# The first eight expert blocks planned and loaded one batch earlier, and the weight splits and the bias fold moved into the last loop body

## The reference, cut to what matters

```
x = x + linear_attention(layernorm(x))            # 16 heads of width 8, prefix sums of Chebyshev polynomials
f = layernorm(x)
f = f + causal_attention(layernorm(f, g1, b1))    # 16 heads, softmax
h = layernorm(f, g2, b2)                          # 8192 tokens x 128
logits = h @ gate_W + gate_b                      # 8 experts
top_v, top_i = top_k(logits, 2);  w = softmax(top_v)
for e in range(8):
    y_e = gelu(h @ exp_W1[e] + exp_b1[e]) @ exp_W2[e] + exp_b2[e]     # 128 -> 512 -> 128
    out += w_full[:, e] * y_e                     # w_full is zero except at the two chosen experts
x = x + f + out
```

## Time and profile before

| | us |
|---|---|
| median of three runs | 1423.27 |
| the three runs | 1413.66, 1423.27, 1428.15 |
| profiled execution, first to last instruction (span) | 1342.0 |
| of it the pipeline over batches, to PE's last product of it | 0 to 1022 |
| PE without work between the pipeline and the first block | 1022 to 1040.5 |
| expert blocks, first hidden product to the second layer's last product | 1043 to 1293.5 |
| last scatters, pairs, sum and store | 1293.5 to 1342 |

### The profile page before, as it was taken

One profiled execution on the slowest core, in us unless ns is written; L12 is line 12 of the kernel. 1 busy time (PEld: TensorE's weight loads), 2 busy tenths in 40 slices (PEclk: granted clock), 3 DMA queues, 4 the chain that ended last, 5 costly groups with the idle time before them and its releaser, 6 DMA issues.

```text
span 1342.0 us, 27933 instructions
## 1 busy us (share of the span) xinstructions
PE 1131.7 (84%) x8883; PEld 706.3 (53%) x8883; DVE 1101.1 (82%) x2555; ACT 938.9 (70%) x1859; POOL 845.8 (63%) x1105
## 2 busy tenths in 40 slices
PE   4576799899999999899998999998891999999950
PEld 1233355554655545555555555554460788888840
DVE  4648889899999999999999999877615788888845
ACT  3243387687877978878777687686664799999940
POOL 3776656778778787777877777532323266666660
PEclk8657799999999999999999999899995899999985
DMA  9131221414325133242341322413431222222239
GB/s 223 40 90 49 53 73 34 122 54 85 90 42 122 66 73 94 58 101 79 61 110 44 83 78 54 109 57 80 152 127 58 79 82 76 93 79 82 67 142 375
DMA packets 84436, 121.91 MB, mean 91 GB/s; under 512 B 15270, under 2 KB 66522, under 8 KB 80002
## 3 DMA queue, kind: packets, MB, share of 16 engines
q1 hardware_dynamic: 70978, 98.07, 27.5%
q0 software_dynamic: 9088, 17.33, 3.9%
q10 hardware_dynamic: 4224, 4.72, 1.0%
HBM read 63.96 MB, written 57.46 MB: 90 GB/s over the span
## 4 chain that ended last, share of the span: by engine, by line
PE 49%; DVE 17%; POOL 12%; issue 9%; ACT 8%; DMA 4%; POOLq 1%; ACTq 0%; SPq 0%; DVEq 0%
PE front L1621 8%; PE back L1633 8%; DVE nm L619 7%; PE back L1487 5%; POOL xg L1217 4%; PE scores L1468 4%; PE front L1353 4%; ACT pr L1006 3%; PE maxima L1428 3%; POOL F L1173 2%; PE scores L1470 2%; DMA stack<-pairs 2%; DVE front L570 2%; POOL F L1174 2%; PE maxima L1430 2%
## 5 line engine op out<-in xcount | busy, mean ns | idle before, releaser
L619 DVE TENSOR_REDUCE nm<-maxima 128x1 f32<-128x384 f32 (+3 forms) x704 | 419.4, 632 | 48.1 <-PE maxima L1430 44.2
L1006 ACT ACTIVATE pr<-scores 128x384 f32<-128x384 f32 (+1 forms) x768 | 373.5, 524 | 105.6 <-PE scores L1470 88.3
L1428 PE MATMUL maxima<-stack 65*128 65x128 bf16 (+2 forms) x768 | 199.5, 283 | 38.0 <-DVE nm L619 34.9
L1468 PE MATMUL scores<-stack 65*128 65x384 bf16 (+2 forms) x768 | 205.9, 280 | 21.7 <-ACT pr L1006 18.1
L1217 POOL DMA_INDIRECT xg<-rows,sloti x128 | 133.0, 1039 | 130.0 <-ACT rows L1027 43.4
L1430 PE MATMUL maxima<-stack 128*128 128x128 bf16 x1024 | 181.4, 225 | 1.5 <-DVE nm L619 1.0
L1470 PE MATMUL scores<-stack 128*128 128x128 bf16 x1024 | 181.1, 223 | 0.0
L1487 PE MATMUL back<-pr,vaug 128*9 128x512 f32 (+3 forms) x2048 | 179.9, 452 | 0.0
L1292 POOL DMA_INDIRECT pairs<-xs x104 | 111.1, 1069 | 78.8 <-DVE xs L852 52.1
L1468 PEld LDWEIGHTS scores<-stack 65*128 65x128 bf16 x768 | 75.6, 98 | 135.6 <-ACT pr L1006 93.7
L1428 PEld LDWEIGHTS maxima<-stack 65*128 65x128 bf16 x768 | 75.2, 99 | 129.2 <-DVE nm L619 85.1
(11 more groups left out here) (219 smaller groups left out, 2466.9 us busy)
## 6 DMA issues: line engine op xcount, KB each, us to landing
stack<-spread SPq DMA_DIRECT2D x32, 400.0 KB
spread<-qs SPq DMA_DIRECT2D x96, 128.0 KB
spread<-ks SPq DMA_DIRECT2D x96, 128.0 KB
stack<-spread SPq DMA_DIRECT2D x32, 384.0 KB
xs<-xg SPq DMA_DIRECT2D x39, 272.0 KB, 2.8
stack<-pairs SPq DMA_DIRECT2D x8, 1024.0 KB, 16.7
stack<-in_consts SPq DMA_DIRECT2D x4, 1280.0 KB
xg<-xs SPq DMA_DIRECT2D x17, 272.0 KB, 2.3
```

Source lines behind the costliest of these rows:

```text
L619: v.tensor_reduce(nm[:, h:h + heads, t], ring(n)[:, 0:heads * (t + 1) * P].rearrange("p (h n) -> p h n", h=heads), AX.X, ALU.max, negate=T ...
L1006: a.activation(pr[:, n % PR, 0:width], ringE[n % 2][:, 0:width], ACT.Exp).then_inc(W.exp_ready, 1)
L1428: k.matmul(ring(n)[:, at:at + t * P], qst[p][0:OPEN_ROWS, h, own], kst[p][0:OPEN_ROWS, h, 0:t * P], start=(j == 0), stop=True, skip_group_ ...
L1468: k.matmul(dst[:, at + P:at + T - t * P], kst[p][0:OPEN_ROWS, h, own], qst[p][0:OPEN_ROWS, h, (t + 1) * P:T], start=(t == tiles[0]), stop= ...
```

## The change

1. **Plan in two halves.** After batch 14's slots DVE plans eight blocks (`EARLY`) from the counts so far, rounded down, so that they are full of rows of batches 0 to 14 (`early_plan`, in the body before the last, slot 65). The other 31 are planned as before, less what is taken (`late_plan`), after the last body and behind block 0's weights and `second_x(0)`.
2. **Rows loaded early.** SP loads six blocks (`AHEAD`) at the head of the last body, behind the filler rows and ahead of batch 15's store; two more behind that store; from block 8 on it waits for the second plan and for batch 15's rows.
3. **Splits earlier.** In the last body ACT makes six experts' first parts ahead of `apply3` (before: none), DVE seven second parts ahead of `gate_top` (before: one); none is left behind the body. `w1_sb` gets its own place over `F`, so that DVE's second parts no longer overwrite it.
4. **Bias fold later.** The 32 products leave the scores of batch 15 and stand in the last body on PE: 12 behind `output2`, 6 behind the gate, 14 behind the ranks. DVE adds them up at its slot 66.
5. **Waits.** PE no longer waits for the whole plan and all 16 second parts; it waits for `b1_ready` ahead of the first hidden product.

```diff
-        w1_sb = qst[0].rearrange("p h n -> p (h n)").bitcast(F32).rearrange("p (e n) -> p e n", e=E)
+        w1_sb = nc.alloc_sbuf_tensor_at("w1_raw", [P, E, HID], F32, offset=place["F"])
...
-        SPLIT_DVE, SPLIT_ACT = (20, 36, 45, 52), (17, 24, 58, 64, 76, 80, 84, 87)
+        SPLIT_DVE, SPLIT_ACT = (6, 8, 10, 12, 14, 16, 18, 34), (2, 4, 6, 8, 10, 12, 22, 40)
+        FOLD_PE = ((10, 12), (44, 6), (60, E * HC - 18))
...
             def body(t, b, m, g, h, f, p, w):
+                if t == B - 1:
+                    sp.wait_ge(W.plan_ready, 1)
+                    sp.wait_ge(W.tail_set, 16 * (2 * E + 1))
+                    sp.wait_ge(W.rows_free, B)
+                    sp.wait_ge(W.acc_set, 16 * (B - 1))
+                    for i in range(AHEAD):
+                        load_rows(i)
...
-            sp.wait_ge(W.plan_ready, 1)
             sp.wait_ge(W.acc_set, 16 * B)
-            sp.wait_ge(W.rows_free, B + 1)
-            for i in range(BLOCKS):
-                at = sp.value_load(plani[0:1, 0, i:i + 1], min_val=0, max_val=E * REGION)
+            for i in range(AHEAD, BLOCKS):
+                if i == EARLY:
+                    sp.wait_ge(W.plan_ready, 2)
+                    sp.wait_ge(W.rows_free, B + 1)
                 if i >= XT:
                     sp.wait_ge(added[i % 2], added_by(i - XT))
-                sp.dma_start(xt[i % XT], xg[bass.ds(at, NB), :].rearrange("(p t) c -> p (t c)", t=QT)).then_inc(xt_loaded[i % XT], 16)
+                load_rows(i)
...
+            def early_plan():
+                v.memset(taken[:, 1:4, :], 0.0).then_inc(W.p_step, 1)
+                v.tensor_scalar(number, cst[:, C_BN:C_BN + BLOCKS], float(NB), None, ALU.mult).then_inc(W.p_step, 1)
+                dve.wait_ge(W.p_step, 3)
+                whole_blocks(3, -0.5 + 0.5 / NB)
+                v.tensor_scalar(upto_taken, upto, float(EARLY), None, ALU.min).then_inc(W.p_step, 1)
+                place_blocks(9, 0, EARLY)
...
+                    if t == B - 2 and n == 65:
+                        early_plan()
+                    if t == B - 1 and n == 66:
+                        first_bias()
...
+            dve.wait_ge(W.plan_ready, 1)
             now = dve.value_load(plani[0:1, 1, 0:1], min_val=0, max_val=E - 1)
             take_w1(0, now)
             second_x(0)
+            late_plan()
...
-                if b == B - 1 and n >= TILES - E * HC:
-                    fold_bias(n - (TILES - E * HC))
...
+                    if b is None and t is not None:
+                        for i, (place, many) in enumerate(FOLD_PE):
+                            if n == place:
+                                first = sum(m for _, m in FOLD_PE[:i])
+                                for j in range(first, first + many):
+                                    fold_bias(j)
...
-            pe.wait_ge(W.plan_ready, 1)
-            pe.wait_ge(W.wl_ready, 2 * E)
...
+                if n == 0:
+                    pe.wait_ge(W.b1_ready, 1)
```

More of the change, by code:

```diff
@@ L254, in block_kernel @@
         mine = lambda k: flat[:, (XT + 1) * QT * RW + k * T:(XT + 1) * QT * RW + (k + 1) * T]
-        scraps = pr[:, 0, :]
-        at_least = x2t[:, :, :].rearrange("p t d -> p (t d)")[:, 0:BLOCKS * E].rearrange("p (n e) -> p n e", e=E)
-        plan = scraps[:, 0:BLOCKS * 4].rearrange("p (k n) -> p k n", k=4)
+        planned = ha[:, :, :].rearrange("p t d -> p (t d)")
+        at_least = outT[:, 0:BLOCKS * E].rearrange("p (n e) -> p n e", e=E)
+        plan = planned[:, 120:120 + BLOCKS * 4].rearrange("p (k n) -> p k n", k=4)
+        taken = planned[:, 280:280 + 4 * E].rearrange("p (k e) -> p k e", k=4)
         gel = [mine(k) for k in range(GS)]
@@ L702, in second_weights, with first_bias @@
                                 w2p[0][:, e * HC:(e + 1) * HC, :], ALU.subtract).then_inc(W.wl_ready, 1)
+            def first_bias():
+                dve.wait_ge(W.b1_mm, 1)
+                v.tensor_tensor(b1p[:, :], X[:, 0:E * HC], col[:, V_EB:V_EB + E * HC], ALU.add).then_inc(W.b1_ready, 1)
+            count, full, upto = (nblk[:, i, :] for i in range(3))
+            upto_taken, next_taken, per_expert, at_first = (taken[:, i, :] for i in range(4))
+            expert, behind, first_row, number = (plan[:, i, :] for i in range(4))
@@ new lines, in whole_blocks @@
+            def whole_blocks(done, rounding):
+                v.tensor_tensor(count, filled_to[:, :], cst[:, C_RG:C_RG + E], ALU.subtract).then_inc(W.p_step, 1)
+                dve.wait_ge(W.p_step, done + 1)
+                v.tensor_scalar(count, count, 1.0 / NB, rounding, ALU.mult, ALU.add).then_inc(W.p_step, 1)
+                dve.wait_ge(W.p_step, done + 2)
+                v.tensor_scalar(full, count, HALF, HALF, ALU.add, ALU.subtract).then_inc(W.p_step, 1)
+                dve.wait_ge(W.p_step, done + 3)
+                v.tensor_tensor_scan(upto, one[:, 0:1].to_broadcast((P, E)), full, 0.0, ALU.mult, ALU.add).then_inc(W.p_step, 1)
+                v.tensor_scalar(per_expert, full, -float(NB), float(REGION), ALU.mult, ALU.add).then_inc(W.p_step, 1)
+                dve.wait_ge(W.p_step, done + 5)
@@ new lines, in place_blocks @@
+            def place_blocks(done, ahead, many):
+                own, cut = at_least[:, 0:many, :], slice(0, many)
+                v.tensor_tensor(own, cst[:, C_BN:C_BN + many].unsqueeze(2).to_broadcast((P, many, E)),
+                                upto.unsqueeze(1).to_broadcast((P, many, E)), ALU.is_ge).then_inc(W.p_step, 1)
+                dve.wait_ge(W.p_step, done + 1)
+                v.tensor_reduce(expert[:, cut], own, AX.X, ALU.add).then_inc(W.p_step, 1)
+                dve.wait_ge(W.p_step, done + 2)
+                v.tensor_tensor(own, own, per_expert.unsqueeze(1).to_broadcast((P, many, E)), ALU.mult).then_inc(W.p_step, 1)
+                v.tensor_scalar(plani[:, 1, ahead:ahead + many], expert[:, cut], float(E - 1), None, ALU.min).then_inc(W.p_step, 1)
+                dve.wait_ge(W.p_step, done + 4)
+                v.tensor_reduce(behind[:, cut], own, AX.X, ALU.add).then_inc(W.p_step, 1)
+                dve.wait_ge(W.p_step, done + 5)
+                v.scalar_tensor_tensor(first_row[:, cut], behind[:, cut], at_first[:, 0:1], number[:, cut], ALU.add, ALU.add).then_inc(W.p_step, 1)
+                dve.wait_ge(W.p_step, done + 6)
+                v.tensor_scalar(plani[:, 0, ahead:ahead + many], first_row[:, cut], float(E * REGION), None, ALU.min).then_inc(W.plan_ready, 1)
@@ new lines, in late_plan @@
+            def late_plan():
+                dve.wait_ge(W.p_step, 16)
+                whole_blocks(16, 0.5 - 0.5 / NB)
+                v.tensor_tensor(upto, upto, upto_taken, ALU.subtract).then_inc(W.p_step, 1)
+                v.scalar_tensor_tensor(per_expert, next_taken, float(NB), per_expert, ALU.mult, ALU.add).then_inc(W.p_step, 1)
+                v.tensor_scalar(at_first, upto_taken, float(NB), None, ALU.mult).then_inc(W.p_step, 1)
+                dve.wait_ge(W.p_step, 24)
+                place_blocks(24, EARLY, BLOCKS - EARLY)
@@ L857, in _ @@
             second_x(0)
+            late_plan()
             for i in range(BLOCKS + 2):
                 for c in range(HC):
+                    if c == 0 and i + 1 == EARLY:
+                        dve.wait_ge(W.plan_ready, 2)
                     if c == 0 and i + 1 < BLOCKS:
```

44 lines of the change are left out of this document (10 added, 34 removed).

## The result

The changed kernel ran in 1406.23 us in the median of 8 runs (1401.52 to 1412.06), the kernel before in 1421.74 (8 runs, 1413.66 to 1428.15): a ratio of 0.9897, interval 0.9866 to 0.9929. Two later comparisons gave 0.9958 (0.9931 to 0.9985) and 0.9912 (0.9879 to 0.9944); the mean of the three is 0.992, some 11 us. Forecast: 1408, 14.9 us less.

What follows compares the result with a forecast made beforehand. The expert blocks were taken as PE-bound, their start held by a chain of waits for batch 15's rows. Block 0 15.9 us earlier, less 1.0 for the late plan, gives 14.9: 1423.3 to 1408 us, range 1400 to 1418.

Steps and rivals of the forecast that it cites:

- The early rows start the blocks: Block 0: its rows are there in time; first hidden product at 1027.2 instead of 1043.08, 15.9 us earlier.
- Rival 3: SP's head waits end late, so early rows don't start the blocks; gain shrinks to 2 us, 1421; chance 0.04.
- The fold leaves the scores: Batch 15's scores: without the 32 fold products on PE, ACT's `hn` is done 3.3 us earlier, at 1001.5.
- POOL is late next: Batch 15's first POOL work stands behind batch 14's dispatches, so starts only 2.0 us earlier (bounds 0.4 and 3.3).
- The splits on this path … I take 0: Batch 15's body: six first parts on ACT hidden, seven second parts on DVE cost 0 (bounds 0 and 0.7 us).
- rival 4: Beside the blocks, DVE's copies hold up POOL's batch 15 dispatches, making block 8's rows late: slower; chance 0.04.
- The last 14 fold products 4.7 us: PE, behind the ranks and ahead of block 0: three products slow, eleven fast, 4.7 us, to 1024.8.
- The late plan 1.0 us: DVE ahead of block 1: block 1 begins 7.6 us after block 0, before 6.65; cost 1.0 us (bounds 0.4 and 2).
- Behind that, nothing: Behind block 1's start: batch 15's dispatches, the scatters, the moved store and block 8's load cost nothing more.
- the smaller gain: PE at half clock through the last 14 products, POOL free no earlier than 1006.2: 11.7 us, 1412; chance 0.16.

Runs made afterwards that it cites:

- second execution of before: The kernel before, unchanged, profiled a second time; time 1410.95 us, span 1409.1 us.
- no early rows: Changed kernel, but first blocks' rows load only when all of batch 15's rows have landed, late plan ahead of block 0; ratio to before 1.0029.
- the execution that I summed on: The kernel before, unchanged, in the profiled execution the prediction started from; span 1342.0 us.
- all moved: Changed kernel with fold in 26 and 6, splits moved off the root, late plan spread, block 0's expert read before the gate; 1400.24 us, ratio 0.9874.

## Why the prediction held, and which steps of it did not

Against the second execution of before, the three executions of the changed kernel have the first product 15.2 us earlier (mean 54.7 against 69.9), block 3 12.2 earlier, the end 11.5 earlier. The forecast had 15.9, then 14.9 and 14.9.

1. *The early rows start the blocks: right, and without them there is no gain* ("no early rows"). SP issued the six loads from 1072.45 to 1078.40, block 0's first: 14.5 us ahead of its transposes, where a load took 2.71 us from issue to landing in the earlier trace rows. Rival 3 is out.

```profile
1072.45 5.95 SPq L390 DMA_DIRECT2D xs<-xg  x6
```

2. *The fold leaves the scores, `hn` 3.3 earlier: right in kind, 2.2 in the mean.* The three executions with the fold in the scores have `hn` at 30.2 in the mean, the ten without at 28.0. The single ones overlap (28.6 to 31.3 against 26.5 to 30.3), so the runs don't tell 2.2 from the 3.3.
3. *"POOL is late next": wrong.* The residual sum waits for DVE's `x2t` (3.74 us above), as the row of before also said (4.09) and I argued away. I also counted the landing, 2.3 to 3.7 us, from the end of the last dispatch's row (1003.70) where it counts from the start (1002.74), as in the earlier trace rows: POOL was free up to 1 us sooner than I took. All of `hn`'s gain passed on: the root begins at 32.5 in the mean of the ten and at 35.3 in the three, 2.8 us against the 2.0 taken. That is more than `hn` gained, because of a step that I had not looked at, `output2` on PE (`front<-wp_sb,hn`), between `hn` and `x2t`. In the three it took 2.1 us, at the half clock; in six of the ten 1.16, at the full one, and there the root begins 4.2 us behind `hn` instead of 5.1. The row of before that goes with the 1.16 above:

```profile
1004.83 2.08 PE L1512 MATMUL front<-wp_sb,hn 128*128 128x128 f32 x8 [0.69 <-ACT hn L1014]
```

4. *"The splits on this path … I take 0": the step that failed.* I counted what the seven splits take on DVE and not whom they hold up. On DVE the forecast was right: the seventh ended at 1080.20, with the gate's products. But the six ahead of it lengthen POOL's root from 3.55 to about 8.1 us, on the path: 4.5 us where the bounds were 0 and 0.7. I had asked whether DVE holds POOL up only for the dispatches (rival 4), and these it hardly did: 0.96 to 1.26 us each, eight in 10.3 us.
5. *The last 14 fold products 4.7 us: the clock as forecast, the price of one product too high, 3.7.* In the first profile of the change the clock rose after the first two or three of them, as the sum had it:

```profile
1083.30:1084.40 1.10, 1.10 (x9) 1.10 (x7) 0.89 (x5) 1.10 (x1) 0.00 (x0) 0.53 0.02 7
1084.40:1087.00 2.60, 2.60 (x26) 2.60 (x25) 1.08 (x2) 0.31 (x2) 1.50 (x2) 1.00 0.71 173
```

But a product in a row of them takes less than a fourth of a gate: the 12 at the full clock took 2.84 us (0.24 each; I took 0.29), the six at half 2.77 (0.46; I took 0.52), and these 14 3.88, 3.72 of it ahead of the transposes. In the other two executions all 14 ran at a granted clock of 1.00 and took 3.2 us. Behind them came 2.9 us to the first product instead of 2.4: DVE needed 0.84 us between `b1p` and the copies to read the expert, which I had not priced.
6. *The late plan 1.0 us: too little.* Block 1 followed 7.70 us after block 0 (7.32 in the other two executions), forecast 7.6. But with the plan spread out it follows after 5.57: the comparison with 6.65 in before hid that before's block 0 was at half clock (0.79 for its first product) while the changed kernel's begins at the full one (0.50). Block 2's transposes come 10.0 us after the first product against 8.2, which is 1.9 us, and 1.1 more are lost up to block 3; the clock had fallen again there (0.51 from 1098 to 1101.5 in the first execution). Up to block 3 the change thus gives back 3.0 us in the mean and not 1.0.
7. *Behind that, nothing: right within what can be seen.* From block 3 to the end it is 293.8 us in before's second execution, 295.0, 296.2 and 292.1 in the changed kernel.

So the time came out near the forecast although the ranks end only 0.3 us earlier than in the second execution (48.7 in the mean against 49.0; forecast 1.9): the root ate what the fold gave. Against the execution that I summed on (46.4) they even end 2.3 us later, an error of 4.2 us. Two things covered for it, and that is luck: behind the ranks the first product came 1.1 us sooner than forecast (6.0 us instead of 7.1), and before's own first product is 2.4 us later in the second execution than in the one I summed on. Against that one the gain in the first product is 12.8 us and not 15.2. The late plan's 2 us more then make 12.2 of the 14.9 up to block 3, and the first comparison is the one of the three with the largest gain. Of the rivals, the smaller gain (1412, 11.7 us) is nearest to the mean of the three comparisons, but not by its mechanism: the clock rose early in the 14 products or was full in all of them, and POOL was not late.

## What to carry to other kernels

Work that fits into an engine's idle time isn't free if it slows the engine that the path is waiting for in that time: before filling VectorE's gap with operations on two SBUF operands, ask what runs on GpSimd in it. A row's named releaser should be overruled only with another row. And a sum made on one execution inherits what is peculiar to it: where the span and the timed runs differ by more than the parts of the sum, look at a second one first.

## What the hardware showed that I had not expected

- POOL's 128x4 operations: 0.20 us beside DVE operations with one PSUM operand, 1.1 us beside those with two in SBUF. Behind the power, POOL gets through one operation for each pair of splits (1.27 us): in all seven executions with the splits beside the root, each of these operations ends 0.04 to 0.10 us behind the end of a pair's second operation (L485 at 1071.26, DVE's row from 1070.53 at 1071.21) and none behind that of a pair's first. Why at the one and not at the other, no run shows.
- The read of an index into DVE's register cost 0.84 us where DVE had been waiting just before, and nothing visible where it lay ahead of the gate ("all moved": copies 0.1 us after the bias).
- A clock held up in one place fell in the next, in one execution: with PE kept busy up to the ranks, the gate ran at the full clock and block 0 had products at half. That the one comes in place of the other isn't shown: executions with the gate at half clock have such products in block 0 or block 1 as well (the changed kernel above: 0.57 from 1091 to 1095).
